# Where the double steps, the exponentials and the low parts stand in a 32-step schedule of fused attention and convolution

## The chip, the cores and the metric

One core of one Trainium2 chip runs the whole program. The metric is the device time in microseconds of that core. The kernel before takes 2341.36 us, the median of three runs (2339.72 to 2341.66). The execution that the profiler recorded took 2340.45 us, and the trace spans 2338.5 us of it.

## The reference, cut to what matters

Layer 0 is self-attention over the 4096 pixels of each of four images with 256 channels, with queries and keys of 32 channels:

```python
q = einsum('qc,bcn->bqn', Wq, xf); k = einsum('qc,bcn->bqn', Wk, xf); v = einsum('vc,bcn->bvn', Wv, xf)
attn = softmax(einsum('bqn,bqm->bnm', q, k) / sqrt(32), axis=-1)
out = gamma[0] * einsum('oc,bchw->bohw', Wo, einsum('bvm,bnm->bvn', v, attn)) + x
```

Layer 1 splits each 8x8 patch of that result into a low part (the mean of 2x2 pixels) and a high part (the rest), puts each through a 1x1 convolution (the high one over itself and itself rolled by one row), then an affine normalisation and a PReLU, and adds the two up again:

```python
low = prelu(bn(mag_w @ mean2x2(p) + mag_b)); high = prelu(bn(phase_w @ concat(high, roll(high)) + phase_b))[:, :C]
y = up2(low) + high
```

## The kernel before, in words

A turn handles one chunk of 512 queries against the 4096 keys of its image. There are 8 turns to an image and 32 in all. The values are multiplied by Wo beforehand and kept as an fp16 high part `uh` and an fp16 low part `ul`; the probabilities are kept in the same two parts.

**Units.** The keys are 32 tiles of 128. Half of them are weighed by direct units `("d", i)`: TensorE multiplies the keys with the queries into bank S (`scores`, L590), ScalarE takes the exponential twice, into fp16 `ph` (L758) and fp32 `p32` (L761), VectorE forms the low part `pl` (`low_probabilities`, L1047), and TensorE weighs with 12 matmuls (`weigh_tile`, L631 to L633). The other half was already scored, with queries on the partitions, by the maximum pass of the turn before, and was kept in 16 blocks of `saved`. These are the kept units `("k", k)`: ScalarE takes two exponentials of a kept block (`slot_probabilities`, L769 and L770), VectorE forms its low part (`slot_low_probabilities`, L1052), SyncE issues a transposing DMA from `pq` to `pt` (`turn_slot`, L372), and TensorE weighs the block with 12 matmuls (`weigh_slot`, L644 to L646). The list `UNITS` has one unit for each of the 32 steps t of a turn: six direct ones, then kept and direct ones in turn (kept unit k at step 6 + 2k up to k = 9), then the kept units 10 to 15 at steps 26 to 31.

**The maximum pass.** During a turn TensorE also computes 32 score tiles of the next queries (`max_scores`, L519), one a step from step 3 on and two in the steps listed in `DOUBLE`. VectorE takes the row maximum of each: of the first 16 with a plain reduction (L943), of the last 16 while it copies them into `saved` (L947). After the last one it forms the negated maxima (`maxima`, L952 to L956), TensorE turns these round (`negmax_rows`, L525), and VectorE finishes the next queries `qcur` (`start_q`, L960, and `finish_q`, L965).

**The other tasks.** A `Plan` hangs further TensorE tasks on steps: the projections of another chunk, "kq" and "u" (steps 0 and 2, in the 24 turns of the plan FULL alone), the transposed output "y" with the residual (5 and 6, or 4 and 5), the low convolution "low" (20 and 21, or 20) and the two halves of the high convolution "high" (22 and 24). FULL serves 24 turns, LAST the next 7, FINAL the last.

**Two banks in turn.** Every such task and every maximum writes bank `M[n % 2]`, where n is its place in the plan's order. Before it TensorE waits on `m_free[n % 2]` until all earlier uses of this bank were taken out. Maxima and "y" are taken out by VectorE, "kq" and "u" by ScalarE and then VectorE, "low" and "high" by ScalarE alone (`norm_low`, L788, `norm_high`, L794).

**The order on each engine** is written out by hand and is the order of a loop over the steps. At step t:

- TensorE does the scores of the direct unit two ahead, which wait for the exponentials of the unit two before (`probs_ready`), then the plan's tasks (at t = 0 these come first), then the unit itself.
- ScalarE does the exponentials of direct unit i + 2, then the kept block k with `EXP_AT[k] == t`, then takes out the plan's tasks; at t = 0 the exponentials of direct unit 2 and the rounding of the queries come after all these.
- VectorE does the low part of the direct unit of step t + 1, at `SCAN` the scan of an input chunk (`scan`, L900), the plan's tasks, the low part of the kept block k with `LOW_AT[k] == t`, and at `QUERIES` the copy `start_q`.
- SyncE handles `turn_slot` 0 to 15 with the other transfers between them. Kept block k uses buffer k mod 4 of `pq` and `pt`; its exponentials wait until the block four before has been transposed.

Of the kernel before, what the change touches and what calls it, by code (L numbers as in the profile page):

```python
# [41 lines left out]
LEAD = 2  # L42


ROUND_X, ROUND_CONV, SCAN, NEGATIVE, QUERIES = 9, 14, 20, 26, 27

DOUBLE = (11, 13, 15, 16, 18, 25)

ND, NK = MT // 2, MT // 2
TURNED = range(NCH // 2, NCH)  # L50
RING = 4
RISE = 6
# [2 lines left out]
    UNITS += [("k", i), ("d", RISE + i)]  # L55
UNITS += [("k", k) for k in range(ND - RISE, NK)]
AT = {unit: t for t, unit in enumerate(UNITS)}
EXP_AT = [AT["k", k] - 5 for k in range(NK)]
LOW_AT = [AT["k", k] - (3 if k < ND - RISE else 4) for k in range(NK)]


MAXIMA = [(j, m) for j in range(SUB) for m in range(NCH) if m not in TURNED] + [(j, m) for m in TURNED for j in range(SUB)]
# [2 lines left out]
def slot_of(j, m):  # L65

    return (m - TURNED[0]) * SUB + j
# [18 lines left out]
def steps_with_maxima(steps, negmax_after=1):  # L86
# [3 lines left out]
    while left:  # L90
        for _ in range(2 if t in DOUBLE else 1):
            j, m = left.pop(0)
            assert m not in TURNED or t > LOW_AT[slot_of(j, m)]
            steps.setdefault(t, []).append(("max", j, m))
# [19 lines left out]
def attention_conv(nc, x, wqk, wv, wo, phase_w, mag_w, params, gamma, alpha, out, q_dram):  # L114
# [7 lines left out]
    with ctx:  # L122
# [123 lines left out]
        def emptied(eng, plan, g, *tasks):  # L246

            for task in tasks:
                n = plan.number[task]
                eng.wait_ge(m_free[n % 2], use(plan, g, n) + 1)  # L250
# [75 lines left out]
        def _(sp):  # L326
# [13 lines left out]
            def fetch_q(slot):  # L340

                for s in range(3):
                    src = q_dram[slot] if isinstance(slot, int) else q_dram[slot].rearrange("k q n -> (k q) n")
                    sp.dma_start(qraw[s * DQK:(s + 1) * DQK, :], src).then_inc(qraw_loaded, 16)
# [22 lines left out]
            def turn_slot(g, k):  # L367

                sp.wait_ge(slot_low, NK * g + k + 1)
                sp.wait_ge(k_weighed, NK * g + k + 1)  # L370
                sp.sem_inc(turn_seen, 1)
                sp.dma_start_transpose(pt[:, k % RING, :, :], pq[:, k % RING, :, :].rearrange("p v n -> p (v n)"))\  # L372
                    .then_inc(turned[k % RING], 16)
# [6 lines left out]
            def load_direct_u(g, m):  # L380

                sp.wait_ge(d_weighed, ND * g + SUB * (m + 1))
                load_u(m, u_direct_loaded)

            def load_turned_u(g, m):

                sp.wait_ge(k_weighed, NK * g + slot_of(SUB - 1, m) + 1 + RING)
                load_u(m, u_turned_loaded)

            def turn(g, parity, c, plan, scans, ends_image=False):  # L390
                slot = c if isinstance(c, int) else ds(c, 1)
                flat = (lambda dram: dram[slot]) if isinstance(c, int) else (lambda dram: dram[slot].rearrange("k q n -> (k q) n"))
                if plan is FULL:

                    sp.wait_ge(x_split[0], EVEN_FIRST + g)
                    gk = (g + 1 + NCH) % ALL
                    sp.dma_start(xb[:, :, :], x_v[ds(gk // NCH, 1), ds(gk % NCH, 1)]).then_inc(xb_loaded, 16)
                    sp.wait_ge(qsave_ready, NCH + g + 1)
                    sp.dma_start(flat(q_dram), qsave[96:128, :]).then_inc(qsave_free, 16)
                turn_slot(g, 0)  # L400
                if plan is not FINAL:

                    sp.wait_ge(qst_ready, g + 2)
                    if plan is FULL:
                        sp.wait_ge(qsave_free, 16 * (NCH + g + 2))
                    fetch_q((c + 2) % NCH if isinstance(c, int) else ds((c + 2) % NCH, 1))
                turn_slot(g, 1)
                if plan is FULL:
                    emptied(sp, plan, g, ("u", 1))
                    sp.dma_start(flat(uh_dram), uh_next_flat[:, :]).then_inc(u_stored, 16)  # L410
                    sp.dma_start(flat(ul_dram), ul_next_flat[:, :]).then_inc(u_stored, 16)
                sp.wait_ge(out_ready, g + 1)
                gp = (g + (ALL - 2)) % ALL
                sp.dma_start(out_v[ds(gp // NCH, 1), ds(gp % NCH, 1)], z[:, :, :]).then_inc(out_stored, 16)
                turn_slot(g, 2)
                if ends_image:
                    sp.wait_ge(u_stored, 32 * g + 64)
                    sp.sem_inc(turn_seen, 1)
                    load_direct_u(g, 0)
                turn_slot(g, 3)  # L420

                emptied(sp, plan, g, ("y", 1))
                if scans:
                    gs = (g + 2 * NCH) % ALL
                    sp.dma_start(xr[:, :, :], x_v[ds(gs // NCH, 1), ds(gs % NCH, 1)]).then_inc(xs_loaded, 16)
                else:
                    sp.dma_start(xr[:, :, :], x_v[ds(g // NCH, 1), ds(g % NCH, 1)]).then_inc(xr_loaded, 16)
                turn_slot(g, 4)
                if ends_image:
                    load_direct_u(g, 1)  # L430
                turn_slot(g, 5)
                turn_slot(g, 6)
                if ends_image:
                    load_turned_u(g, TURNED[0])
                turn_slot(g, 7)
                turn_slot(g, 8)
                if ends_image:
                    load_direct_u(g, 2)
                turn_slot(g, 9)
                turn_slot(g, 10)  # L440
                if ends_image:
                    load_turned_u(g, TURNED[1])
                turn_slot(g, 11)
                if scans:
                    sp.wait_ge(xs_scanned, g + 2)
                    sp.dma_start(xr[:, :, :], x_v[ds(g // NCH, 1), ds(g % NCH, 1)]).then_inc(xr_loaded, 16)
                turn_slot(g, 12)
                turn_slot(g, 13)
                if ends_image:
                    load_direct_u(g, 3)  # L450
                turn_slot(g, 14)
                turn_slot(g, 15)
                if ends_image:
                    load_turned_u(g, TURNED[2])
                    load_turned_u(g, TURNED[3])

            turns(sp, turn, image_end=lambda g, parity, c, scans: turn(g, parity, c, FULL, scans, ends_image=True))
            sp.wait_ge(out_ready, ALL + 1)
            sp.dma_start(out_v[B - 1, NCH - 2], z[:, :, :]).then_inc(out_stored, 16)
# [235 lines left out]
        def _(act):  # L695
# [67 lines left out]
            def slot_probabilities(g, k):  # L763

                if k == 0:
                    act.wait_ge(bias_ready, g + 1)
                act.wait_ge(turned[k % RING], 16 * (NK // RING * g + k // RING + 1))
                bias = nbias[:, k % SUB:k % SUB + 1]
                nc.scalar.activation(pq[:, k % RING, 0, :], saved[:, k, :], ACT.Exp, scale=SCALE, bias=bias)  # L769
                nc.scalar.activation(saved[:, k, :], saved[:, k, :], ACT.Exp, scale=SCALE, bias=bias).then_inc(slot_probs, 1)  # L770
# [32 lines left out]
            def turn(g, parity, c, plan, scans):  # L803
# [8 lines left out]
                for t, (unit, i) in enumerate(UNITS):  # L812
                    if t > 0 and unit == "d" and i + LEAD < ND:
                        probabilities(g, i + LEAD)
                    for k in range(NK):
                        if EXP_AT[k] == t:
                            slot_probabilities(g, k)
# [40 lines left out]
        def _(dve):  # L858
# [190 lines left out]
            def slot_low_probabilities(g, k):  # L1049

                dve.wait_ge(slot_probs, NK * g + k + 1)
                nc.vector.tensor_tensor(pq[:, k % RING, 1, :], saved[:, k, :], pq[:, k % RING, 0, :],  # L1052
                                        ALU.subtract).then_inc(slot_low, 1)
# [48 lines left out]
            def turn(g, parity, c, plan, scans):  # L1102
# [6 lines left out]
                for t in range(MT):  # L1109
# [13 lines left out]
                    for k in range(NK):  # L1123
                        if LOW_AT[k] == t:
                            slot_low_probabilities(g, k)
# [141 lines left out]
```

## Time and profile before

| | before |
|---|---|
| median of 3 runs | 2341.36 us |
| profiled execution, its span | 2340.45 us, 2338.5 us |
| TensorE matmuls busy | 2205.9 us (94% of the span) |
| VectorE busy | 1782.4 us (76%) |
| ScalarE busy | 1431.6 us (61%) |
| GpSimd busy | 677.7 us (29%) |
| mean granted TensorE clock | 0.984 of full speed |

A matmul's end is modelled in the trace, so one matmul overlaps the start of the next one. A row of the timeline gives start, duration, engine, line, operation, tiles and count, and in brackets how long the engine had been idle and what ended the idle time. "PE" is TensorE, "DVE" VectorE, "ACT" ScalarE, "POOL" GpSimd and "SPq" the SyncE queue.

### The profile page before, as it was taken

To read this page: it belongs to the slowest core of one execution; us is meant where nothing else is said; L and a number is where in the kernel's file an instruction comes from. 1 tells how busy PE (TensorE), PEld (TensorE's weight loads), DVE (VectorE), ACT (ScalarE), POOL (GpSimd) and SP (SyncE) were. 2 spreads that over 40 slices of the span, in tenths; PEclk is the share of its full clock that TensorE was granted. 3 is DMA by queue.
4 is the path that set the end of the run, shared out by engine and by line. 5 is a ranking of instruction groups with operands and counts; after the bars stand their busy time and mean duration, and the time that the engine had idled before them with its cause. 6 is when DMAs were issued, how large, how long until landed. Compare 5 with 4: busy or idle time off the path is not lost.

```text
span 2338.5 us, 48099 instructions
## 1 busy us (share of the span) xinstructions
PE 2205.9 (94%) x16373; PEld 1764.1 (75%) x16373; DVE 1782.4 (76%) x3388; ACT 1431.6 (61%) x2547; POOL 677.7 (29%) x891
## 2 busy tenths in 40 slices
PE   5799999999989999999998999999999999999997
PEld 4577777777767777777777777777777777777776
DVE  6777877777867788877786877777877777778764
ACT  3457666657656666666656666566665656666663
POOL 3232332232322323322232321323322232233321
PEclk8799999999999999999999999999999999999998
DMA  4254444454554444444474443443445444344443
GB/s 159 59 115 94 99 109 102 84 117 99 135 131 85 110 107 92 109 108 97 93 168 102 99 99 72 104 96 91 103 111 133 75 89 93 77 82 88 84 86 64
DMA packets 596617, 235.02 MB, mean 101 GB/s; under 512 B 547072, under 2 KB 548352, under 8 KB 596576
## 3 DMA queue, kind: packets, MB, share of 16 engines
q1 hardware_dynamic: 596576, 234.51, 45.5%
q8 instruction: 22, 0.36, 0.1%
q14 instruction: 19, 0.16, 0.0%
HBM read 67.67 MB, written 32.53 MB: 43 GB/s over the span
## 4 chain that ended last, share of the span: by engine, by line
PE 64%; DVE 15%; issue 10%; DMA 5%; ACT 3%; POOL 1%; SPq 1%; DVEq 0%; ACTq 0%; POOLq 0%
PE M L482 13%; PE M L519 7%; PE O L631 7%; PE O L633 6%; PE O L632 6%; PE O L644 6%; PE O L646 6%; PE O L645 6%; DVE pq L1052 5%; DMA pt<-pq 4%; PE S L590 4%; DVE saved L947 4%; DVE pmax L943 2%; DVE pl L1047 2%; PE M L500 1%
## 5 line engine op out<-in xcount | busy, mean ns | idle before, releaser
L758 ACT ACTIVATE ph<-S 128x512 f16<-128x512 f32 x512 | 307.6, 601 | 525.5 <-PE S L590 524.8
L644 PE MATMUL O<-uh,pt 128*128 128x257 f16 x2048 | 568.2, 277 | 16.9 <-DMA pt<-pq 16.7
L631 PE MATMUL O<-uh,ph 128*128 128x257 f16 x2048 | 570.3, 278 | 4.5 <-DVE pl L1047 4.1
L633 PE MATMUL O<-uh,pl 128*128 128x257 f16 x2048 | 563.2, 275 | 0.0
L632 PE MATMUL O<-ul,ph 128*128 128x256 f16 x2048 | 561.8, 274 | 0.0
L646 PE MATMUL O<-uh,pt 128*128 128x257 f16 x2048 | 559.0, 273 | 0.0
L645 PE MATMUL O<-ul,pt 128*128 128x256 f16 x2048 | 555.7, 271 | 0.0
L947 DVE TENSOR_SCALAR_CACHE_REDUCE saved<-M 128x512 f32<-128x512 f32 x512 | 344.0, 687 | 257.0 <-PE M L519 253.0
L1047 DVE TENSOR_TENSOR pl<-p,ph 128x512 f16<-128x512 f32 x512 | 402.6, 787 | 60.5 <-ACT p L761 59.1
L519 PE MATMUL M<-kst,qst 96*128 (+1 forms) x1024 | 424.0, 442 | 20.9 <-DVE saved L947 16.2
L1052 DVE TENSOR_TENSOR pq<-saved,pq 128x512 f16<-128x512 f32 x512 | 387.6, 757 | 19.2 <-ACT saved L770 19.1
L943 DVE TENSOR_REDUCE pmax<-M 128x1 f32<-128x512 f32 (+1 forms) x512 | 341.4, 684 | 70.8 <-PE M L519 67.8
L769 ACT ACTIVATE pq<-saved,nbias 128x512 f16<-128x512 f32 x512 | 369.2, 721 | 1.3 <-DMA pt<-pq 1.3
L770 ACT ACTIVATE saved<-saved,nbias 128x512 f32<-128x512 f32 x512 | 367.9, 719 | 0.0
L761 ACT ACTIVATE p<-S 128x512 f32<-128x512 f32 x512 | 307.7, 601 | 0.0
L631 PEld LDWEIGHTS O<-uh,ph 128*128 128x128 f16 x2048 | 201.1, 98 | 133.7 <-issue 92.6
L644 PEld LDWEIGHTS O<-uh,pt 128*128 128x128 f16 x2048 | 198.8, 97 | 121.1 <-issue 52.4
L1215 POOL TENSOR_TENSOR zlow<-zlow,zlneg 128x256 f32<-128x256 f32 x32 | 23.8, 744 | 797.5 <-DVE zneg L1067 797.5
L590 PE MATMUL S<-qcur,kst 128*128 128x512 f32 x512 | 238.1, 475 | 16.5 <-ACT p L761 14.1
L519 PEld LDWEIGHTS M<-kst,qst 96*128 96x128 f32 x1024 | 188.3, 191 | 60.8 <-DVE saved L947 27.1
L633 PEld LDWEIGHTS O<-uh,pl 128*128 128x128 f16 x2048 | 201.7, 98 | 26.1
L646 PEld LDWEIGHTS O<-uh,pt 128*128 128x128 f16 x2048 | 197.8, 97 | 29.2
(161 smaller groups left out, 2907.4 us busy)
## 6 DMA issues: line engine op xcount, KB each, us to landing
xr<-in_x SPq DMA_DIRECT2D x53, 512.0 KB, 3.8
out_y<-z SPq DMA_DIRECT2D x33, 512.0 KB, 3.0
xb<-in_x SPq DMA_DIRECT2D x25, 512.0 KB, 3.7
pt<-pq SPq DMA_TRANSPOSE x512, 3.1
qraw<-q_scratch SPq DMA_DIRECT2D x99, 64.0 KB, 2.0
uh_scratch<-uh_next SPq DMA_DIRECT2D x24, 257.0 KB, 3.2
uh<-uh_scratch SPq DMA_DIRECT2D x24, 257.0 KB, 3.2
ul_scratch<-ul_next SPq DMA_DIRECT2D x24, 256.0 KB, 3.1
```

Source lines behind the costliest of these rows:

```text
L519: return nc.tensor.matmul(bank[:, :], qst[0:96, j * 128:(j + 1) * 128], kst[0:96, keys_at], start=True, stop=True)
L631: nc.tensor.matmul(O[j][:, 0:UW], ph[:, i % 4, q], uh[:, i, :], start=(i == 0), stop=False)
L632: nc.tensor.matmul(O[j][:, 0:C], ph[:, i % 4, q], ul[:, i, :], start=False, stop=False)
L633: ins = nc.tensor.matmul(O[j][:, 0:UW], pl[:, i % 4, q], uh[:, i, :], start=False, stop=False)
L644: nc.tensor.matmul(O[j][:, 0:UW], pt[:, k % RING, i, :], uh[:, t, :], start=False, stop=False)
L645: nc.tensor.matmul(O[j][:, 0:C], pt[:, k % RING, i, :], ul[:, t, :], start=False, stop=False)
L646: ins = nc.tensor.matmul(O[j][:, 0:UW], pt[:, k % RING, SUB + i, :], uh[:, t, :], start=False, stop=(ends and i == SUB - 1))
L769: nc.scalar.activation(pq[:, k % RING, 0, :], saved[:, k, :], ACT.Exp, scale=SCALE, bias=bias)
L943: nc.vector.tensor_reduce(pmax[:, j, ds(m, 1)], bank[:, :], AX.X, ALU.max).then_inc(free, 1)
L947: nc.vector.tensor_scalar(saved[:, slot_of(j, m), :], bank[:, :], 0.0, None, ALU.add, ALU.max, accum_out=pmax[:, j, m:m + 1]).then_inc(fre ...
L1047: nc.vector.tensor_tensor(pl[:, i % 4, :], p32[:, i % 2, :], ph[:, i % 4, :], ALU.subtract).then_inc(lo_ready, 1)
L1052: nc.vector.tensor_tensor(pq[:, k % RING, 1, :], saved[:, k, :], pq[:, k % RING, 0, :], ALU.subtract).then_inc(slot_low, 1)
```

## The change

Four groups of constants and the place of one call are changed. The work itself and its instructions stay the same; only their order on the engines changes.

```diff
-ROUND_X, ROUND_CONV, SCAN, NEGATIVE, QUERIES = 9, 14, 20, 26, 27
-DOUBLE = (11, 13, 15, 16, 18, 25)
+ROUND_X, ROUND_CONV, SCAN, NEGATIVE, QUERIES = 9, 14, 22, 26, 28
+DOUBLE = (9, 13, 17, 22, 24, 26)
...
-EXP_AT = [AT["k", k] - 5 for k in range(NK)]
-LOW_AT = [AT["k", k] - (3 if k < ND - RISE else 4) for k in range(NK)]
+EXP_AT = [AT["k", k] - 6 for k in range(NK)]
+LOW_AT = [AT["k", k] - 4 for k in range(NK)]
...
                     sp.dma_start(flat(ul_dram), ul_next_flat[:, :]).then_inc(u_stored, 16)
+                turn_slot(g, 2)
                 sp.wait_ge(out_ready, g + 1)
                 gp = (g + (ALL - 2)) % ALL
                 sp.dma_start(out_v[ds(gp // NCH, 1), ds(gp % NCH, 1)], z[:, :, :]).then_inc(out_stored, 16)
-                turn_slot(g, 2)
```

`DOUBLE` holds six steps before and after, so the last maximum stays at step 28. The exponentials of kept block 0 move from step 1 to step 0, those of block 1 from 3 to 2, and so on to block 15, from step 26 to 25. The low parts of blocks 0 to 9 move one step forward (block 0 from 3 to 2, block 1 from 5 to 4), those of blocks 10 to 15 stay.

## Rows read from the trace of the kernel before

**Rows 1.** Windows, a FULL and a LAST turn: busy us (instructions) per engine, clock, DMA.

```profile
1020.20:1089.80 69.60, 67.80 (x512) 54.40 (x511) 55.24 (x103) 44.43 (x79) 20.45 (x27) 1.00 0.46 102
...
1924.40:1990.10 65.70, 63.33 (x482) 50.29 (x481) 50.58 (x99) 40.91 (x74) 18.20 (x23) 1.00 0.41 83
```

**Rows 2.** Waits of the whole run, TensorE: total us, times, longest us.

```profile
PE M L525 <- DVE nmax L954: 21.4, 32, 1.7
...
PE O L644 <- DMA pt<-pq: 16.7, 29, 2.7
```

**Rows 3.** Timeline, TensorE, later steps of two turns (FULL, then LAST).

```profile
1043.41 0.28 PE L644 MATMUL O<-uh,pt 128*128 128x257 f16 x1 [0.40 <-DMA pt<-pq]
...
1049.18 0.51 PE L519 MATMUL M<-kst,qst 96*128 x1 [0.19 <-DVE pmax L943]
...
1057.08 0.50 PE L519 MATMUL M<-kst,qst 96*128 x1 [0.38 <-DVE saved L947]
...
1070.65 0.39 PE L519 MATMUL M<-kst,qst 96*128 x1
1070.89 0.28 PE L644 MATMUL O<-uh,pt 128*128 128x257 f16 x1
...
1086.55 0.62 PE L525 MATMUL M<-ident,nmax 128*128 128x128 f32 x4 [0.35 <-DVE nmax L954]
...
1932.23 0.28 PE L631 MATMUL O<-uh,ph 128*128 128x257 f16 x1 [0.23 <-DVE pl L1047]
...
1958.18 0.49 PE L519 MATMUL M<-kst,qst 96*128 96x512 f32 x1 [0.17 <-DVE saved L947]
...
1986.85 0.62 PE L525 MATMUL M<-ident,nmax 128*128 128x128 f32 x4 [1.67 <-DVE nmax L954]
```

**Rows 4.** Timeline, ScalarE, start of a FULL turn.

```profile
1022.67 0.62 ACT L776 ACTIVATE kst<-M 96x512 f32 x1
...
1025.00 0.60 ACT L761 ACTIVATE p<-S 128x512 f32<-128x512 f32 x1
...
1026.95 0.73 ACT L769 ACTIVATE pq<-saved,nbias 128x512 f16<-128x512 f32 x1
...
1028.17 0.60 ACT L758 ACTIVATE ph<-S 128x512 f16<-128x512 f32 x1
...
1029.12 0.71 ACT L781 ACTIVATE uh_next<-M,uscale 128x512 f16<-128x512 f32 x1
```

**Rows 5.** Timeline, TensorE, start of the same turn.

```profile
1026.38 0.48 PE L590 MATMUL S<-qcur,kst 128*128 128x512 f32 x1
...
1031.71 0.29 PE L631 MATMUL O<-uh,ph 128*128 128x257 f16 x1
```

**Rows 6.** Timeline, VectorE, start of the same turn.

```profile
1029.87 0.75 DVE L1079 SCALAR_TENSOR_TENSOR ul_next<-M,uscale,uh_next 128x512 f16<-128x512 f32 x1 [1.10 <-ACT uh_next L781]
1030.53 0.68 DVE L1047 TENSOR_TENSOR pl<-p,ph 128x512 f16<-128x512 f32 x1
...
1031.73 0.68 DVE L1052 TENSOR_TENSOR pq<-saved,pq 128x512 f16<-128x512 f32 x1
```

**Rows 7.** Timeline, ScalarE, after the first half of the high convolution.

```profile
1070.93 0.78 ACT L794 ACTIVATE z<-M,bnB,bnA 128x512 f32<-128x512 f32 x1 [2.01 <-PE M L482]
1071.61 0.71 ACT L769 ACTIVATE pq<-saved,nbias 128x512 f16<-128x512 f32 x1
```

**Rows 8.** DMA issues of the whole run: count and median us to landing.

```profile
pt<-pq SPq DMA_TRANSPOSE x512, 3.1
```

**Rows 9.** Timeline, VectorE, later steps of the same turn.

```profile
1042.09 1.04 DVE L1052 TENSOR_TENSOR pq<-saved,pq 128x512 f16<-128x512 f32 x1
...
1071.08 0.69 DVE L947 TENSOR_SCALAR_CACHE_REDUCE saved<-M 128x512 f32<-128x512 f32 x1 [3.22 <-PE M L519]
...
1084.16 0.94 DVE L960 CAST qcur<-qst 96x512 fp32r<-96x512 f32 x1
1085.03 0.68 DVE L947 TENSOR_SCALAR_CACHE_REDUCE saved<-M 128x512 f32<-128x512 f32 x1
```

## The prediction

> **What bounds the kernel now.** I read the page first: TensorE is the busiest engine, and the chain that ended last runs mostly over it. Then I cut the run into turns with the windows view. A FULL turn lasts 69.6 us with TensorE busy for 67.8, a LAST turn 65.7 us with 63.3, both at the full granted clock [rows 1]. VectorE has 55 us of work in a turn and ScalarE 44, so neither bounds a turn as a whole. TensorE works through a fixed order, so anything that makes it wait adds to the end, and any wait taken away shortens it. The question is therefore which waits inside one turn go and which come.
>
> The waits view names those of TensorE [rows 2], and the timeline places them. A wait's lateness is a little more than its printed idle time, because modelled ends overlap: the maximum at 1070.65 is printed with 0.39 us, yet its follower starts 0.24 us later. I add this 0.15 to each idle time [rows 3]. A FULL turn then has these waits that the change touches:
>
> - Kept unit 2 waits for its transposed block at 1043.41: 0.40 + 0.15 = 0.55.
> - The second maximum of step 13 waits at 1049.18: 0.19 + 0.15 = 0.34.
> - The maximum of step 17, behind the doubles of 15 and 16, waits at 1057.08: 0.38 + 0.15 = 0.53.
> - The turned maxima wait for `nmax` at 1086.55: 0.35 + 0.15 = 0.50.
>
> That is 1.92 us a turn. In a LAST turn the step 17 wait is 0.32 and the one for `nmax` 1.82 [rows 3].
>
> **What the change removes.** With the low part of kept block 2 a step earlier, its transposition is issued earlier by about that step. The call moved ahead of the output store helps too; the store that it passes has to be done only when ScalarE overwrites `z` with the high convolution at 1070.93 [rows 7], long after, so I cost that at nothing. The 0.55 goes. With the doubles of 11 to 18 thinned out to 9, 13 and 17, VectorE has, between two doubles, a pair of steps with four operations, and the two waits of 0.34 and 0.53 go. `QUERIES` at 28 takes the copy `start_q` from before the last maximum to behind `maxima`: the last maximum was taken out at 1085.03 behind that copy, which began at 1084.16 [rows 9]. Without it VectorE is free 0.87 earlier. The new double at 26 puts one more maximum (0.6) before it in VectorE's queue than before, but TensorE comes later by 0.24 too. Walking the queue from step 26 on (two maxima, a low part, the negative parts, a maximum, a low part) I find 0.1 of the 0.87 used up by that double, so `nmax` comes 0.77 earlier against TensorE. In FULL the whole 0.50 goes; in LAST 0.77 of 1.82. The scan at 22 falls into the time in which VectorE waited 3.22 us for the high convolution [rows 9], so it is free. Before, at step 20, it held nobody up either.
>
> Gain: 1.92 in FULL; 0.32 + 0.77 = 1.09 in LAST.
>
> **What the change adds at the start of a turn.** Here ScalarE, not TensorE, is short of time: from the first exponential it is busy without a break for the first 12 us. Kept block 0 costs it 1.22 us, from 1026.95 to 1028.17 [rows 4]. Its exponentials now stand before the copy of the keys at 1022.67, and so before the exponentials of direct unit 2, whose second one starts at 1025.00. That becomes 1026.22, and it is done at 1026.82. TensorE starts the scores of direct unit 4, which wait for it, at 1026.38 [rows 5]; they now start at 1026.87. First loss: 0.49.
>
> Then block 1. ScalarE has done the same total of work by the exponentials of direct unit 4, so these are not later. But block 1 now comes at step 2, ahead of the copy of the second "u" half, which moves from 1029.12 to 1030.34 [rows 4]. VectorE waited 1.10 us for that copy before `ul_next` at 1029.87 [rows 6]. It now starts at 1031.08. Behind it stands the low part of kept block 0 (0.60), moved from step 3 to step 2, and only then the low part of direct unit 4: 1031.08 + 0.66 + 0.61 = 1032.35, done at 1033.03. TensorE weighed that unit from 1031.71 on, or from 1032.20 with the first loss [rows 5]. Second loss: 0.87 with the latency of a signal. The scores behind it wait too, since TensorE goes in order. The start costs 1.36 in FULL.
>
> In a LAST turn no "u" stands in the way, but TensorE is already waiting for the low part of direct unit 3 at 1932.23 [rows 3]. The chain before it (exponentials of unit 2, its low part, the normalisation, the low queries) has no slack, so the 1.22 passes through almost whole: 1.2.
>
> **What the change adds at the high convolution.** This depends on the two banks. Counted out with the new `DOUBLE`, in FULL the first half of "high" is n = 29 and the maxima of step 22 are n = 30 and 31. So the second maximum of the double needs the bank that "high" has just filled, and it waits for ScalarE. At step 24 it is n = 33 and then 34, 35: the same. LAST has 25 with 26, 27 and 29 with 30, 31. Before, one maximum stood there, in the other bank, and the next one came a whole unit later. The trace shows the price: a maximum behind "high" starts at 1070.65 and should be followed by a second one 0.24 later, at 1070.89 [rows 3], but ScalarE takes "high" out from 1070.93 to 1071.61 [rows 7]. With the signal that is 1071.70 at the earliest, or 0.81; I take 0.75 as the first maximum's own switch may overlap.
>
> The Trainium skill, "PSUM — Partial Sum Buffer", section "PSUM bank collisions raise a hardware error", says that the engines must be kept apart by bank with semaphores, since nothing else does. By that rule the wait can't be shortened, and the sum stays the same; the trace agrees in so far as no matmul here enters a bank before it is taken out.
>
> At step 24 ScalarE has kept block 14 ahead of "high", and its exponentials wait until block 10 is transposed. The low part of block 10 stands at the end of step 22 behind the late second maximum, by my walk 4.6 us before the second half of "high" is through. A transposition lands after 3.1 us [rows 8], the exponentials take 1.22: 4.3 in all, and the issue and its signals come on top. "high" is taken out 0 to 0.4 late; I take 0.2. The two double steps cost 0.75 + 0.75 + 0.2 = 1.70.
>
> **The sum.** FULL: 1.36 + 1.70 - 1.92 = +1.14. LAST: 1.20 + 1.70 - 1.09 = +1.81. FINAL has no maxima: it has the late start (+1.2) and waits for two transposed blocks less (about as much), so 0. In all 24 x 1.14 + 7 x 1.81 = 27.4 + 12.7 = 40. On the profiled execution's 2340.45 us that is 2380, and on the median, 0.9 us higher, 2381. The 0.2 for the transposition at step 24 is the least sure term and may be nothing; counted at its half it takes 31 x 0.1 = 3 us off. I forecast **2377**.
>
> **Bounds.** An operation of VectorE with two SBUF inputs takes 0.68 us alone [rows 6] and 1.04 beside GpSimd [rows 9]. The double at step 9 falls into the time in which GpSimd splits the frequencies. A pair of steps with a double has five VectorE operations, 3.05 us, or 3.8 with two of them slowed, against 3.6 for TensorE. The slack of the pair before absorbs this once; if it doesn't, up to 0.5 a turn is lost. The Trainium skill, "SBUF — State Buffer", section "Who interferes with whom", says that a VectorE instruction with two SBUF inputs contends with a GpSimd one that reads SBUF, while a reduction doesn't. By that rule the maxima themselves are never slowed, only the low parts between them; the trace agrees in the 1.04 above.
>
> **Rivals.**
>
> 1. *The start costs only the first loss.* If the copy of "u" is not behind block 1 in time, or VectorE's low part is not late, 0.87 falls away in FULL: 2377 - 21 = 2356. Against it: the order on both engines is plain in the code, and VectorE already waits 1.10 there.
> 2. *VectorE becomes the bound in the middle.* The contention costs 0.4 in each of 31 turns: 2377 + 12 = 2389. For it: five operations against 3.6 us. Against it: before, the double at 11 lay under GpSimd too and cost nothing.
> 3. *The doubles at 22 and 24 wait for nobody*, if the second maximum's bank were free: the turn then costs 1.36 - 1.92 = -0.56 in FULL and 1.20 - 1.09 = +0.11 in LAST, in all -13: 2341 - 13 = 2328, faster. It decides the sign as soon as the two waits are below 0.28 each in FULL. Against it: the count of n. For it: VectorE and ScalarE both have long idle times there.
> 4. *ScalarE's start is absorbed wholly*, because TensorE would have waited at those places for something else: 2377 - 24 x 1.36 - 7 x 1.2 = 2336, no change that can be told.
>
> **Chances.** The forecast 0.42; rival 1 0.16; rival 2 0.20; rival 3 0.15, with everything else on the faster side; rival 4 0.07. So slower 0.78, within 0.2% 0.07 (about 4.7 us, what a measurement of this kernel can tell from no change), faster 0.15. The range from 2335 to 2398 leaves out rival 3 and the far end of rival 2. The slower cases alone lie between 2350 and 2398.
>
> **What would show it.** In the profile after: TensorE L590 waiting for ScalarE L761 by about 0.5 at the third step of a FULL turn, and L631 waiting for VectorE L1047 two steps later; L519 waiting for ScalarE L794 twice a turn, which it never did; the waits of L644 for the transposed block 2 and of L519 for `pmax` and `saved` gone; the wait of L525 gone in FULL and near 1 us in LAST. FULL turns of about 70.7 us and LAST ones of 67.4. The prediction is wrong if L519 shows no wait for L794, or if the first 13 us of a turn are no longer than before.

## The result, and the profile after

The changed kernel takes 2369.8 us (median of 4 runs, 2368.49 to 2371.05) against 2341.51 us before. The ratio is 1.0123, with a 95% interval of 1.0107 to 1.0139: 28 us slower. The forecast was 2377, 36 us slower. The profiled executions differ by 28.9 us in their spans (2367.4 and 2338.5), so the two traces hold the whole difference.

TensorE's work is the same, 2205.1 us busy against 2205.9. The windows view of a FULL and a LAST turn, in the columns of [rows 1]:

```profile
1025.70:1096.25 70.55, 67.76 (x511) 54.62 (x511) 53.98 (x103) 44.42 (x79) 22.04 (x28) 1.00 0.45 100
2010.00:2077.40 67.40, 63.63 (x482) 50.26 (x481) 49.49 (x100) 40.99 (x74) 18.31 (x24) 1.00 0.40 81
```

A FULL turn takes 0.95 us longer with the same busy time and the same clock, a LAST turn about 1.75. The waits of TensorE in the changed kernel show where:

```profile
PE M L519 <- ACT z L794: 44.6, 62, 0.8
PE O L631 <- DVE pl L1047: 20.5, 48, 0.6
PE S L590 <- ACT p L761: 20.4, 25, 6.2
...
PE M L525 <- DVE nmax L954: 8.0, 8, 1.3
...
PE O L644 <- DMA pt<-pq: 0.9, 2, 0.7
```

The first line did not exist before: 62 times, twice in each of 31 turns, a maximum waits for ScalarE to take "high" out. The wait for `nmax` fell from 32 times to 8, the one for a transposed block from 16.7 us to 0.9 [rows 2]. The timeline of TensorE in a FULL turn gives the places:

```profile
1025.98 0.63 PE L482 MATMUL M<-xbh,wkq 128*128 128x512 f32 x2
...
1032.32 0.51 PE L590 MATMUL S<-qcur,kst 128*128 128x512 f32 x1 [0.24 <-ACT p L761]
...
1038.55 0.28 PE L631 MATMUL O<-uh,ph 128*128 128x257 f16 x1 [0.62 <-DVE pl L1047]
...
1072.29 1.20 PE L482 MATMUL M<-hh,wp 128*128 128x512 f32 x4 [0.49 <-ACT zlow L788]
...
1075.19 0.39 PE L519 MATMUL M<-kst,qst 96*128 x1
1076.30 0.50 PE L519 MATMUL M<-kst,qst 96*128 x1 [0.72 <-ACT z L794]
```

The first row is the first projection and the fourth the high convolution. In the trace of before they stand at 1020.52 and 1067.75:

```profile
1020.52 0.63 PE L482 MATMUL M<-xbh,wkq 128*128 128x512 f32 x2
...
1067.75 1.20 PE L482 MATMUL M<-hh,wp 128*128 128x512 f32 x4 [0.49 <-ACT zlow L788]
```

Measured from the first projection, the fifth scores come 6.34 us on (5.86 before, [rows 5]) and the weighing of direct unit 4 comes 12.57 us on (11.19 before): the start costs 0.48 and then 1.38 in all. From there to the high convolution 33.74 us pass, against 36.04 before. Two maxima fewer stand in that stretch (0.47), so 1.83 us of waits went. From the high convolution to the end of the turn it is 24.24 against 22.37: the two maxima more, two new waits, and the wait for `nmax` less. The three differences, +1.38, -2.30 and +1.87, make the 0.95.

The two maxima of the new double are 1.11 us apart, where 0.23 is usual: 0.88 lost, though the row prints 0.72. ScalarE's rows for the same stretch, and for the second high convolution:

```profile
1075.47 0.78 ACT L794 ACTIVATE z<-M,bnB,bnA 128x512 f32<-128x512 f32 x1 [2.02 <-PE M L482]
...
1081.40 0.72 ACT L769 ACTIVATE pq<-saved,nbias 128x512 f16<-128x512 f32 x1 [3.94 <-DMA pt<-pq]
...
1082.65 0.76 ACT L794 ACTIVATE z<-M,bnB,bnA 128x512 f32<-128x512 f32 x1
```

"high" is taken out from 1075.47, and the late maximum starts at 1076.30, after it. At step 24 the exponentials of block 14 do wait for a transposition, 3.94 us of ScalarE's idle time, but they end just as "high" is ready: the delay is nothing.

At the start, ScalarE and VectorE stand as the walk had them:

```profile
1028.14 0.75 ACT L769 ACTIVATE pq<-saved,nbias 128x512 f16<-128x512 f32 x1
...
1031.67 0.60 ACT L761 ACTIVATE p<-S 128x512 f32<-128x512 f32 x1
...
1035.80 0.71 ACT L781 ACTIVATE uh_next<-M,uscale 128x512 f16<-128x512 f32 x1
```

```profile
1036.54 0.75 DVE L1079 SCALAR_TENSOR_TENSOR ul_next<-M,uscale,uh_next 128x512 f16<-128x512 f32 x1 [2.07 <-ACT uh_next L781]
1037.21 0.68 DVE L1052 TENSOR_TENSOR pq<-saved,pq 128x512 f16<-128x512 f32 x1
1037.81 0.68 DVE L1047 TENSOR_TENSOR pl<-p,ph 128x512 f16<-128x512 f32 x1
```

VectorE waits 2.07 us for the copy of the second "u" half, where it waited 1.10 [rows 6]; the low part of block 0 stands next, and only then that of direct unit 4.

### The profile page after: what moved, and what is told of

Same layout as the page of the kernel before. It is cut to its first block, busy times and chain, and to the rows that moved or that the text cites. A ratio compares the mean times of both kernels' runs of the same rounds, so it can differ in the third digit from the quotient of the medians.

```text
span 2367.4 us, 48099 instructions
## 1 busy us (share of the span) xinstructions
PE 2205.1 (93%) x16373; PEld 1767.5 (75%) x16373; DVE 1746.6 (74%) x3388; ACT 1431.5 (60%) x2547; POOL 711.9 (30%) x891
## 4 chain that ended last, share of the span: by engine, by line
PE 66%; ACT 15%; issue 9%; DMA 5%; DVE 4%; POOL 1%; ACTq 1%; SPq 0%; DVEq 0%; POOLq 0%
PE O L644 9%; PE O L646 9%; PE M L519 9%; PE O L645 9%; PE O L631 7%; PE O L633 6%; PE O L632 6%; PE M L482 6%; DMA pt<-pq 4%; PE S L590 3%; ACT saved L770 3%; ACT pq L769 3%; ACT p L761 2%; ACT z L794 2%; ACT ph L758 2%
## 5 line engine op out<-in xcount | busy, mean ns | idle before, releaser
L631 PE MATMUL O<-uh,ph 128*128 128x257 f16 x2048 | 569.4, 278 | 20.9 <-DVE pl L1047 20.5
L519 PE MATMUL M<-kst,qst 96*128 (+1 forms) x1024 | 432.7, 444 | 56.4 <-ACT z L794 44.6
L1047 DVE TENSOR_TENSOR pl<-p,ph 128x512 f16<-128x512 f32 x512 | 379.7, 742 | 75.8 <-ACT p L761 71.3
L1052 DVE TENSOR_TENSOR pq<-saved,pq 128x512 f16<-128x512 f32 x512 | 380.3, 743 | 12.3 <-ACT saved L770 12.2
L519 PEld LDWEIGHTS M<-kst,qst 96*128 96x128 f32 x1024 | 192.7, 191 | 106.6 <-ACT z L794 71.5
L633 PEld LDWEIGHTS O<-uh,pl 128*128 128x128 f16 x2048 | 201.3, 98 | 25.9
```

The lines of the kernel that those rows point to most:

```text
L519: return nc.tensor.matmul(bank[:, :], qst[0:96, j * 128:(j + 1) * 128], kst[0:96, keys_at], start=True, stop=True)
L631: nc.tensor.matmul(O[j][:, 0:UW], ph[:, i % 4, q], uh[:, i, :], start=(i == 0), stop=False)
L633: ins = nc.tensor.matmul(O[j][:, 0:UW], pl[:, i % 4, q], uh[:, i, :], start=False, stop=False)
L1047: nc.vector.tensor_tensor(pl[:, i % 4, :], p32[:, i % 2, :], ph[:, i % 4, :], ALU.subtract).then_inc(lo_ready, 1)
```

## The experiments

Each kernel is an edit of the changed kernel or, where said, of the kernel before. Medians are of 4 runs or more. A difference to the changed kernel is taken from its 2369.8 us. A ratio is to the kernel before as it was timed beside that experiment; its median lay between 2338.7 and 2341.0 us in them, so a difference of 2 or 3 us between two experiments tells nothing.

### The double steps alone

```diff
-DOUBLE = (9, 13, 17, 22, 24, 26)
+DOUBLE = (9, 13, 17, 23, 25, 26)
```

> The changed kernel with the double steps 22 and 24 moved to 23 and 25: DOUBLE = (9, 13, 17, 23, 25, 26). Theory (the second maximum of a double behind the high convolution waits for ScalarE to empty its bank): TensorE's waits of L519 for ScalarE's L794 (44.6 us in 62 waits after the change) go to zero and nothing else changes, 31 turns x 0.88 x 2 = 54 us less, about 2315 us. Rival (the high steps are only where a backlog of VectorE shows, and it shows elsewhere): L519 waits for saved or pmax instead and the time stays above 2355 us.

Measured: 2308.4 us, ratio to the kernel before 0.9868 (0.9852 to 0.9885). That is 61 us less than the changed kernel, from two numbers in the list. L519 waits for L794 no more. Its line is gone, and the others are those of the changed kernel:

```profile
PE S L590 <- ACT p L761: 21.7, 25, 7.3
PE O L631 <- DVE pl L1047: 20.6, 48, 0.6
...
PE M L525 <- DVE nmax L954: 8.1, 8, 1.3
```

One maximum now follows "high", and two come a unit later:

```profile
1050.35 0.39 PE L519 MATMUL M<-kst,qst 96*128 x1
...
1051.84 0.71 PE L519 MATMUL M<-kst,qst 96*128 x2
```

A FULL turn takes 68.57 us instead of 70.53 and a LAST one 65.5 instead of 67.45, 0.98 for each double step. The theory holds; a step costs 0.1 more than the 0.88 between the maxima, since the unit behind a late maximum starts late as well (0.34 us after it instead of 0.24).

### The first two kept blocks

```diff
 LOW_AT = [AT["k", k] - 4 for k in range(NK)]
+EXP_AT[:2], LOW_AT[:2] = [1, 3], [3, 5]
```

> The changed kernel with the exponentials of kept blocks 0 and 1 back at steps 1 and 3 and their low parts at 3 and 5. Theory (ScalarE's order at the start of a turn costs 1.36 us in each of 24 turns and 1.2 in each of 7): 41 us less, about 2329 us, and the waits of L590 and L631 at the start of a turn go. Rival (the start is late for another reason, the late end of the turn before): under 10 us less, about 2360 us or more.

Measured: 2337.4 us, 32 us less than the changed kernel; the ratio to the kernel before is 0.9992 (0.9982 to 1.0001). The usual FULL turn falls from 70.53 to 69.33 and a LAST one from 67.45 to 66.4. The start's waits are gone, and L519 still waits 62 times for "high" (the line numbers are one higher in this kernel):

```profile
PE M L520 <- ACT z L795: 44.1, 62, 0.9
...
PE O L632 <- DVE pl L1048: 4.1, 15, 0.4
```

24 x 1.20 + 7 x 1.05 = 36 us by the turns, 32 by the medians, 41 expected. The cause holds, the size was a tenth to a fifth too large.

### One block at a time

Two kernels, with one line each behind `LOW_AT`:

```diff
+EXP_AT[0] = 1
```

```diff
+EXP_AT[1] = 3
```

> The changed kernel with only the exponentials of kept block 0 back at step 1, its low part left at step 2. Theory (the two losses of the start are one delay counted up to the low part of direct unit 4, which hangs on block 1 and on the low part of block 0): the wait of the fifth scores goes, but the wait at weighing direct unit 4 grows by the same 0.49 us, so the 24 FULL turns keep their length; the 7 LAST turns lose up to 1.2 us each. In all 0 to 9 us less, 2361 to 2370 us. Rival (the two losses add up independently): 24 x 0.49 + 7 x 1.2 = 20 us less, about 2350 us.

> The changed kernel with only the exponentials of kept block 1 back at step 3, its low part left at step 4. Theory: the copy of the second u half is no longer behind block 1, the wait of 0.88 us at weighing direct unit 4 goes from the 24 FULL turns, the first loss of 0.49 stays: 21 us less, about 2349 us. Rival (the low part of block 0 on VectorE is what makes unit 4 late): less than 8 us gained, above 2362 us.

Measured: 2361.4 us for block 0 (8.4 less than the changed kernel) and 2349.3 us for block 1 (20.5 less). With block 0 back, a FULL turn keeps its length, and only LAST turns shorten, from 67.45 to 66.3. The trace of that kernel shows why the 0.48 us of the fifth scores are not saved at all. TensorE comes a little sooner to a maximum whose bank still holds the second "u" half, waits there for VectorE's `ul_next`, and then for the same low part as ever (the line numbers are one higher here too):

```profile
1038.30 0.49 PE L520 MATMUL M<-kst,qst 96*128 x1 [0.38 <-DVE ul_next L1080]
...
1039.41 0.28 PE L632 MATMUL O<-uh,ph 128*128 128x257 f16 x1 [0.62 <-DVE pl L1048]
```

So the losses at the start are for the most part one delay that is paid in two places. A FULL turn gains nothing with block 0 back, 0.88 with block 1 back (69.66 us) and 1.20 with both, so block 1 ahead of the copy of "u" is what it hangs on; in a LAST turn it is block 0. The low part of block 0 has a share as well: at 1037.21 it stands between `ul_next` and the low part of direct unit 4 and takes 0.60 of the way. No kernel puts it back alone.

### Both undone, and a further wait

```diff
-DOUBLE = (9, 13, 17, 22, 24, 26)
+DOUBLE = (9, 13, 17, 23, 25, 26)
...
 LOW_AT = [AT["k", k] - 4 for k in range(NK)]
+EXP_AT[:2], LOW_AT[:2] = [1, 3], [3, 5]
```

> Both undone together on the changed kernel: DOUBLE = (9, 13, 17, 23, 25, 26), and kept blocks 0 and 1 at their steps of before. Theory (two independent losses): the sum of both single results, 61 and 32 us less than the changed kernel, about 2276 us, 2.8% under the kernel before. Rival (each hides part of the other): 2290 us or more.

Measured: 2276.9 us, ratio to the kernel before 0.9725 (0.9708 to 0.9741). The single results, 61.4 and 32.4 us, add up to 93.8, and it is 92.9: the two losses are independent. FULL turns take 67.34 us. What is left of the change is worth 64 us.

The largest wait left in a FULL turn is an old one, of the high convolution for the bank of the second low convolution, which ScalarE takes out behind 1.22 us of exponentials:

```diff
+EXP_AT[11] = 22
```

> As the one before, and the exponentials of kept block 11 at step 22 in place of 21. Theory (the high convolution waits 0.66 us in each of 24 turns because ScalarE has 1.22 us of exponentials ahead of emptying the second low convolution): that wait goes, 16 us less, about 2260 us. Rival (the later exponentials of block 11 only move the delay to emptying the high convolution or to the transposition of block 11): within 4 us of the kernel without it.

Measured: 2256.8 us, 20 us less again; the ratio to the kernel before is 0.9646 (0.963 to 0.9662). The wait for `zlow` is gone from the list, and FULL turns take 66.59 us, 0.75 less, where the expectation had 0.66. This is the fastest version of the study, 3.5% under the kernel before, with TensorE busy for 96% of the span:

```profile
PE 2171.3 (96%) x16373; PEld 1760.8 (78%) x16373; DVE 1736.0 (77%) x3388; ACT 1431.9 (64%) x2547; POOL 725.6 (32%) x891
```

### The copy of the queries

```diff
-ROUND_X, ROUND_CONV, SCAN, NEGATIVE, QUERIES = 9, 14, 22, 26, 28
+ROUND_X, ROUND_CONV, SCAN, NEGATIVE, QUERIES = 9, 14, 22, 26, 27
```

> The changed kernel with QUERIES back at 27. Theory (the copy of the queries ahead of the last maximum makes the turned maxima late by 0.50 us in FULL and 0.77 in LAST): 24 x 0.50 + 7 x 0.77 = 17 us more, about 2387 us, and L525 waits for nmax in every turn. Rival (the late maxima of the steps 22 and 24 leave the end of a turn no slack, or so much that the copy is hidden): under 6 us or over 25 us more.

Measured: 2390.7 us, 20.9 more than the changed kernel. The wait for `nmax` is back in every turn:

```profile
PE M L525 <- DVE nmax L954: 25.9, 32, 1.8
```

It is a little larger than before the change (21.4 us in 32 waits, [rows 2]), since the double of step 26 puts one maximum more ahead of it. That took 0.1 a turn in the prediction and is here some 0.15: a FULL wait prints 0.50 instead of 0.35, a LAST one 1.82 instead of 1.67. The kernel before with the new `DOUBLE` alone (below) has the same 25.9 us in 32 waits, so it is the doubles that add it.

### SyncE's order, and the lead of the low parts

```diff
-                turn_slot(g, 2)
                 sp.wait_ge(out_ready, g + 1)
...
+                turn_slot(g, 2)
                 if ends_image:
```

```diff
-LOW_AT = [AT["k", k] - 4 for k in range(NK)]
+LOW_AT = [AT["k", k] - (3 if 2 <= k < ND - RISE else 4) for k in range(NK)]
```

> The changed kernel with turn_slot 2 back behind the output store. Theory (the store only takes SyncE's issue time, and TensorE is 1.4 us late by then anyway): no change, within 3 us of 2370 us. Rival (the transposition moved behind half a megabyte of output lands late): kept unit 2 waits again, up to 13 us more.

> The changed kernel with the low parts of kept blocks 2 to 9 back at three steps of lead, blocks 0 and 1 as changed. Theory of the prediction (the step of lead removes the wait of kept unit 2 and, with the doubles, those of steps 13 and 17): kept unit 2 waits 0.55 us again in 24 turns, 13 us more, about 2383 us. Rival (TensorE is 1.4 us late by then, which gives the transposition its time whatever the lead): within 4 us of 2370 us.

Measured: with SyncE's order of before 2369.7 us, no difference. With the low parts of blocks 2 to 9 back 2396.0 us, 26 more, more than either theory had. Kept unit 2 does not wait again. Instead, in the turn read, kept units 3 and 4 start 0.50 and 0.47 us after the maximum before them, where the changed kernel has 0.32, so they are 0.19 and 0.15 late, and the second maximum of step 17 is 0.43 late:

```profile
1061.35 0.10 PEld L644 LDWEIGHTS O<-uh,pt 128*128 128x128 f16 x1 [0.34 <-DMA pt<-pq]
```

```profile
1070.71 0.51 PE L519 MATMUL M<-kst,qst 96*128 x1 [0.27 <-DVE pmax L943]
```

The first of these stands in the weight loads: the matmul behind it shows no wait of its own. The late start of the unit behind step 17 (0.11) and a longer wait at the double of step 24 (0.15) make up the rest of the 1.02 us by which this turn is longer. The rival was right on kept unit 2 and wrong on the time, since other units took the wait over.

### Which part took the old waits away

```diff
-DOUBLE = (9, 13, 17, 22, 24, 26)
+DOUBLE = (11, 13, 15, 16, 18, 25)
```

> The changed kernel with DOUBLE = (11, 13, 15, 16, 18, 25) as before. Both theories: the waits behind the high convolution go, 61 us less than the changed kernel, 2309 us. Then theory (the new spacing is what took away the waits of steps 13 and 17): they come back, 24 x 0.87 + 7 x 0.32 = 23 us, about 2332 us. Rival (the earlier low parts took them away): no wait at these steps, about 2309 us, as with the spaced doubles at 23 and 25.

Measured: 2310.9 us. With the doubles of before, and the rest of the change, no wait stands at the steps 13 and 17. It differs from the first experiment, which has the spaced doubles, by 2.6 us. So spacing the doubles is not needed once the low parts are early.

The last two kernels are edits of the kernel before. One has the lead alone, the other the new `DOUBLE` alone:

```diff
+EXP_AT[2:] = [AT["k", k] - 6 for k in range(2, NK)]
+LOW_AT[2:] = [AT["k", k] - 4 for k in range(2, NK)]
```

```diff
-DOUBLE = (11, 13, 15, 16, 18, 25)
+DOUBLE = (9, 13, 17, 22, 24, 26)
```

> The kernel before with one part of the change alone: the exponentials of kept blocks 2 to 15 one step earlier and the low parts of blocks 2 to 9 one step earlier; blocks 0 and 1, DOUBLE, SCAN, QUERIES and SyncE's order as before. Theory (this alone takes away the waits of kept unit 2 and of the steps 13 and 17): 24 x 1.42 + 7 x 0.32 = 36 us less than before, up to 45 as the waits proved larger than their printed idle time, 2296 to 2305 us. Rival (kept unit 2 also needs the moved transposition or a late TensorE, and the maxima need the spaced doubles): 15 us less or under.

> The kernel before with DOUBLE of the change alone. Theory (two waits of 0.99 us a turn behind the high convolution, 61 us, and spacing the doubles takes nothing away that counts): near 2400 us, less at most 5. Rival, the prediction's step (the spaced doubles take away the waits of the steps 13 and 17): 61 - 24 x 0.87 - 7 x 0.32 = 38 us more, about 2378 us.

Measured: the lead alone 2316.9 us, ratio 0.9908 (0.9891 to 0.9924), 22 us faster than before; the doubles alone 2391.1 us, ratio 1.0224 (1.0207 to 1.0241), 52 us slower. Both lie between their theory and their rival. With the lead alone the waits at the steps 13 and 17 are gone, and a FULL turn takes 68.63 us instead of 69.58. But kept unit 2 waits as long as ever, though its low part is a step earlier (the line numbers are two higher in this kernel):

```profile
1032.48 0.28 PE L646 MATMUL O<-uh,pt 128*128 128x257 f16 x1 [0.46 <-DMA pt<-pq]
```

SyncE's rows of the same turn show why. VectorE had the low part of block 2 done at 1027.39, but the transposition stands behind the output store and goes out only at 1028.63:

```profile
1028.03 0.39 SPq L416 DMA_DIRECT2D out_y<-z  x1
1028.63 1.45 SPq L374 DMA_TRANSPOSE pt<-pq  x1
```

In the kernel with both losses undone, TensorE is as early, the low part is done at 1005.04, and the moved call lets the transposition go at 1005.37, ahead of the store:

```profile
1005.37 1.28 SPq L373 DMA_TRANSPOSE pt<-pq  x1
1007.13 0.39 SPq L416 DMA_DIRECT2D out_y<-z  x1
```

Counted from the turned maxima before it, the median issue over FULL turns is 22.95 us on before the change, 22.69 with the lead alone and 21.77 here, and the block has landed 26.4, 26.5 and 25.0 us on. The lead alone moves the landing by nothing.

With the doubles alone, the two new waits cost 61 us by the first experiment, and the turns are 1.54 longer (71.12), so the spacing gives back some 9 us, net of the 4.5 that the wait for `nmax` grows by. Small waits for `pmax` and for transposed blocks are spread over the middle of the turn instead of standing at two steps: by their starts the second maxima of the steps 9, 13 and 17 are 0.16, 0.20 and 0.26 late, kept unit 3 is 0.22 late. Part of what it gives back is at kept unit 2: its block lands no earlier (26.4), and the unit starts as far from the turned maxima as before the change (26.49 and 26.48 in the turns read), but the second maximum of step 9 is now done ahead of it, in what was idle time.

## Why the prediction was right

**The start, 1.36 forecast, 1.38 in the trace.** Both places were where the walk had put them (0.48 and 1.38 in all). Calling them "first loss" and "second loss" was right as a sum for both moves together, but they aren't two costs: the one-block kernels show one delay. Rival 1, the first loss alone, is out, and so is rival 4. What undoing it gave was less, 1.20 in a FULL turn. The traces show most of the last 0.18. In the kernel before, the maximum of step 5 stands right behind VectorE's reduction of the one before:

```profile
1032.93 0.68 DVE L943 TENSOR_REDUCE pmax<-M 128x1 f32<-128x512 f32 x1
...
1033.27 0.60 PE L500 MATMUL M<-ident,oraw 128*128 128x128 f32 x4
1033.76 0.49 PE L519 MATMUL M<-kst,qst 96*128 x1
```

It starts 0.49 after the first transposition of "y". In the changed kernel that distance is 0.36 (1040.11 to 1040.47), and with the two blocks back it is 0.51. So a wait of about 0.14, too short to be printed, hides behind the late start and comes back with it undone.

**The doubles at 22 and 24, 1.70 forecast, 1.96 measured.** Counting n decided the sign of this study. The price is 0.98 for each step, not 0.75: I took 0.06 off for the first maximum's switch, which did not come, had the bank free 0.06 to 0.07 too early, and left out the 0.10 by which the unit behind the pair starts late. The 0.2 for the late transposition at step 24 was nothing. The waits are those of the bank: in every row looked at, the second maximum starts after ScalarE has taken "high" out, as the Trainium skill, "PSUM — Partial Sum Buffer", section "PSUM bank collisions raise a hardware error", asks for. Rival 3, that these waits do not come, is out, and shows what was at stake: without them the kernel is 31 us faster than before.

**The waits taken away, 1.92 forecast, about 2.3 measured in a FULL turn** (1.83 in the middle and 0.50 for `nmax`). I had 1.42 in the middle, from printed idle times and 0.15 each. By their starts, set against the same pairs of matmuls where nothing waits, kept unit 2 was 0.56 late and the maxima of the steps 13 and 17 were 0.34 and 0.54 late, as I had them. What I left out is the unit behind each of the two maxima, which starts another 0.11 and 0.10 late, and the 0.14 of the maximum of step 5, which the late start hides. Some 0.04 is spread. This is the mis-sized term. The late start and the doubles together were put 0.28 too low, the waits taken away 0.4 too low: that the two nearly cancel is luck.

**Which part took them away was wrong.** The prediction gave the waits of the steps 13 and 17 to the thinned doubles. The low parts did it: they now stand in the kept steps, between the maximum of a kept step and those of the direct step behind it. With the old doubles they are just as gone (2310.9 us), and with the old low parts and the new doubles the wait of step 17 is back. The wait of kept unit 2 was given to its earlier low part and the moved call. Alone, the lead does not remove it, and neither move is needed while TensorE is 1.4 us late (the kernels with the call and with the low parts put back; in the second the block lands 26.9 us after the turned maxima and TensorE comes for it at 27.4). Whether the lateness would do without either, and without the new double at step 9, was not tried. With TensorE on time, in the kernel with both losses undone, call and lead are both there and that wait is rare: all waits for a transposed block are 3.6 us in 7. What was missing with the lead alone is the moved call, by SyncE's rows above; no kernel adds it by itself. The scan, moved from step 20 to 22 and put at nothing, was not undone alone either; of the time saved in the middle of a FULL turn, where it stands, the terms above leave 0.04 us unexplained.

**The sum.** From wait to wait of `nmax`, 23 intervals of FULL turns grew by 21.5 us and the seven behind them by 12.3 (forecast 12.7). The first turn became 3.7 us shorter, as a wait of 2.7 us for a transposed block went, and the last turn with the tail 0.9 shorter. With 0.3 less before the first turn that is 28.9. The forecast lay 8 us above this. The usual FULL turn accounts for 4.7 of it (21.5 instead of 23 x 1.14 = 26.2), as the larger removed waits outweigh the dearer doubles; the first turn for 4.8 (-3.7 instead of +1.1); the last turn, the time before the first one and the LAST turns for 1.6; and the 3 us that I had taken off go the other way. The forecast had taken the first turn for a usual one, and it stands 1 us under its own sum, since 2381 less 3 is 2378.

**VectorE as the bound (rival 2)** did not come. The five operations to a pair with a double at step 9 made no wait in the changed kernel.

## What to carry to other kernels

When two banks are used in strict turn, write down n for each task of a step before putting two tasks of one kind there. The second one meets the bank of whatever stands before the first, and here that was worth 61 us in two list entries. Work moved earlier on an engine that has slack on average is still moved ahead of something: look up what follows it in that engine's order, at the one place of the turn where that engine has no slack. And undo parts one by one even when the total came out as forecast, since the parts of this change were +61 and +32 us of loss over 64 us of gain, and the fastest version keeps some parts, puts others back and adds one of its own.

## What the hardware showed that was not expected

The copy `start_q` (L960) took 0.943 us in the median before and 0.410 in the changed kernel, each beside GpSimd's additions to `z` in the turns looked at, and the four-element L954, which stands behind the last maximum in both kernels, 0.429 against 0.214. With `QUERIES` back at 27 in the changed kernel both are long again, 0.942 and 0.430, so they go with the place of the copy, before or behind the last maximum. Why is open. What L954 saves is part of what the wait for `nmax` lost.
